# An attention step reordered: the latent product of the step behind moves up to the scores, the outputs move to the end

## The chip, the cores and the metric

The kernel runs on one core of a Trainium2 chip. The metric is device time in microseconds (us): 2148.81 us is the median of three runs of the kernel before. The core has a matrix engine (TensorE, PE in the rows; its weight loads are PEld), a vector engine (VectorE, DVE), a scalar engine (ScalarE, ACT), GpSimd (POOL) and a queue engine that only issues transfers (SyncE, SP). Each runs its own instruction stream in order and waits for the others on semaphores.

## What is computed

A front end of convolutions gives `h` (16 x 128 tokens of 1024). Then comes the part that the change touches, and then a feed-forward layer with low-rank experts. Cut to the attention:

```
q_c = rmsnorm(x @ w_qa);  q = q_c @ w_qb            # 32 heads, 128 plain + 64 rotary
k_c, k_rope = x @ w_kva;  k_c = rmsnorm(k_c)        # a latent of 128, shared by all heads
q_rope, k_rope = rotary(q_rope), rotary(k_rope)
scores = q_nope . k_nope + q_rope . k_rope          # per batch of 128 tokens and head
attn   = softmax(scores * 192**-0.5)
out    = attn @ v;  h = h + out @ w_o
```

The kernel never forms keys or values. It multiplies each head's query weight by its key weight beforehand (`wp`), and its value weight by its output weight (`m`); the scores are then taken against the latent `kc`, and `attn @ kc` (the latent product) is multiplied by `m` and added to `resid`. All matmuls work on fp16 pairs, a high part and a low part, so each product is three matmuls.

## The kernel before

The attention phase has 32 rounds of 4 steps, 128 steps `s`. A round is a group of 4 heads and a quad of 4 batches; a step is one batch j of the quad, for 4 heads at once. Each engine has a `body` for a round, written out by hand; the order within it is the order of the instructions. Rounds 1 to 26 run in a loop of two rounds a turn, rounds 28 to 30 in a loop of one; rounds 0, 27 and 31 stand alone. `more` is true for rounds 0 to 27.

In one step of before the engines do this.

- PE: `scores` of step s (12 matmuls of 128 columns against the latent, then 8 against the rotary keys, which wait for `zt`); `rope` of step s+1 (9 of 256 columns); `outputs` of step s-1 (24 of 512 columns into two banks); `queries` (9 of 512, one head of the next round); where `more` and j is 1 to 3, `products` (one third of the next group's weight product, in fp32); then the latent product of step s (3 of 512: `av_ps`), which waits for `turned`.
- DVE: the row maximum `mx` and its scaled negative `nmx`; `rotate` (4 instructions, `ra`, `rb`); `rrec` and the division of `prob`; the low half `z` of the rotary query; the low half of `halves`; two residual additions `add_out` for step s-1; `query_low`; `prod_low`; then `ot_l`, the low half of the latent product.
- ACT: at the start of a round the load of the next head's weights (`load`, line 858, 928 KB into `wide`); four exponentials `prob`; the high half of `z`; the high half of `halves`; `query_high`; `prod_high`; then `ot_h`, the high half of the latent product.
- SP: two DMA transposes a step, `zt` (`turn_rope`, the rotary queries of step s) and `turned` (`turn_prob`, both halves of the probabilities of step s). Both go on the SP queue, in the order of the code; the load goes on ACT's.

Single buffers tie the steps together: `halves`, `turned`, `av_ps`, `ot_h`, `ot_l`, `zt`, `z`, `s_ps` exist once. Registers that hold loop positions are worked out on PE's own sequencer, between the matmuls (rows `ISA` and `REGISTER_ALU` below).

Of the kernel before, what the change touches and what calls it, by code (L numbers as in the profile page):

```python
# [27 lines left out]
P = 128  # L28
# [706 lines left out]
def attention_phase(nc, keep, raw_loaded, heads_d):  # L735
# [3 lines left out]
    with ExitStack() as ctx:  # L739
# [60 lines left out]
        @block.sync  # L800
        def _(sp):
            def turn_rope(s):
                waits = [(z_lo, s + 1)]
                if not isinstance(s, int) or s >= 1:
                    waits.append((s_done, s))
                wait_apart(sp, sp_passed, *waits)
                sp.dma_start_transpose(zt[:, :, :], z[:, :, :].rearrange("p h n -> p (h n)")
                                       ).then_inc(zt_turned, 16)

            def turn_prob(s):  # L810
                waits = [(p_lo, s + 1)]
                if not isinstance(s, int) or s >= 1:
                    waits.append((av_done, s))
                wait_apart(sp, sp_passed, *waits)
                sp.dma_start_transpose(turned[:, :, :], halves[:, :]).then_inc(p_turned, 16)

            turn_rope(0)
            turn_prob(0)
            with sp.Fori(1, ROUNDS * QUAD) as s:
                turn_rope(s)  # L820
                turn_prob(s)

        @block.scalar
        def _(act):
# [45 lines left out]

            def body(before, now, after, more):
# [4 lines left out]
                for j in range(QUAD):  # L876
                    s = now.slot + j
                    act.wait_ge(max_step, s * 2 + 2)
# [24 lines left out]
        def _(dve):  # L903
# [61 lines left out]

            def body(before, now, after, more):
                for j in range(QUAD):
                    s = now.slot + j
                    dve.wait_ge(s_done, s + 1)
# [14 lines left out]
                    behind = (now, j - 1) if j else (before, QUAD - 1)  # L984
# [16 lines left out]
                if not after:  # L1001
                    for hf in range(2):
                        add_out(now, QUAD - 1, hf)
                    dve.wait_ge(out_added, ROUNDS * 8)
# [4 lines left out]
        def _(pe):  # L1009
# [103 lines left out]

            def body(before, now, after, more):
                operands = score_operands(now, 0)
                for j in range(QUAD):
                    s = now.slot + j
                    scores(now, j, operands)
                    if after or j < QUAD - 1:
                        if j < QUAD - 1:  # L1120
                            rope(now, j + 1)
                        else:
                            rope(after, 0)
                    if before or j:
                        if j:
                            outputs(now, j - 1)
                        else:
                            outputs(before, QUAD - 1)
# [4 lines left out]
                    if more and j:  # L1133
                        products(now.t + HEADS, now.parity, j - 1, prod_ps, (now.t + HEADS) * 3 + (j - 1))
                    if before or j:
                        pe.wait_ge(o_lo, s)
                    at = bass.ds(now.tok + j * P, P)
                    probs_h, probs_l = (turned[:, at, :].rearrange("p h n -> p (h n)")
                                        for at in (slice(0, HEADS), slice(HEADS, 2 * HEADS)))
                    pe.wait_ge(p_turned, s * 16 + 16)  # L1140
                    pe.matmul(av_ps[:, :], kc_h[:, at], probs_h, start=True, stop=False)
                    pe.matmul(av_ps[:, :], kc_l[:, at], probs_h, start=False, stop=False)
                    pe.matmul(av_ps[:, :], kc_h[:, at], probs_l, start=False, stop=True).then_inc(av_done, 1)
                if not after:
                    outputs(now, QUAD - 1)
# [354 lines left out]
```

## Time and profile before

| | us |
|---|---|
| median of 3 runs | 2148.81 (2148.19 to 2150.49) |
| the profiled execution | 2150.39 |
| its span, first to last instruction | 2148.6 |
| front end, up to the first scores | 518.33 |
| steady rounds 10 and 11 | 43.35 and 42.97 |
| rounds 28, 29, 30 (no weight products) | 43.11, 42.84, 42.39 |
| PE busy in the span | 1956.3 (91%) |

The attention phase begins at 518 us of the span and ends near 1907. The profiled execution lasted 1.8 us longer than its span, which is what lies before the first and after the last instruction. PE's busy time counts modelled ends of matmuls that overlap the next one, so waits of PE under 0.2 us don't show as idle; they do show in the distance between two starts.

### The profile page before, as it was taken

The page shows a single profiled execution, that of the slowest core. Times are in us where ns is not written, and L with a number is a line of the kernel's source. Part 1 is how long each engine was busy: PE and PEld are TensorE (multiplying, and loading weights), DVE is VectorE, ACT ScalarE, POOL GpSimd, SP SyncE. Part 2 cuts the span into 40 slices and gives each one's busy share as a digit, 9 for nine tenths or more (in the row PEclk, how much of TensorE's full clock was granted, in tenths as well). Part 3 has the DMA queues.
Part 4 walks back from the last instruction along what each step waited for, and adds up shares of the span by engine and source line. Part 5 has one row for each costly group of instructions (what it writes and reads, how often), then busy time and mean ns, then how long its engine had stood idle before and what let it go on. Part 6 is the DMA issues. An engine that isn't in the chain of part 4 may idle for free. (4 is left out here: it accounts for less than half of the span.)

```text
span 2148.6 us, 42567 instructions
## 1 busy us (share of the span) xinstructions
PE 1956.3 (91%) x11826; PEld 1066.0 (50%) x11826; DVE 1344.1 (63%) x2822; ACT 792.8 (37%) x2067; POOL 315.4 (15%) x612
## 2 busy tenths in 40 slices
PE   4688888866999999999999999999999999949999
PEld 1344444443555555555555555555555555525554
DVE  3666666654666666666666666666666666655664
ACT  3344444433333333333333333333333333332221
POOL 2355555430000000000000000000000000023332
PEclk8888888978999999999999999999999999979999
DMA  4111111102222222222222222222222121142332
GB/s 136 40 40 39 39 39 39 36 1 81 55 56 55 72 54 53 53 72 54 54 53 71 55 52 54 72 54 54 54 72 54 38 38 37 38 137 70 79 86 70
DMA packets 250560, 123.82 MB, mean 58 GB/s; under 512 B 240272, under 2 KB 240528, under 8 KB 248336
## 3 DMA queue, kind: packets, MB, share of 16 engines
q1 hardware_dynamic: 246192, 94.71, 20.2%
q10 hardware_dynamic: 4320, 28.51, 3.8%
q8 instruction: 25, 0.41, 0.1%
q14 instruction: 23, 0.19, 0.0%
HBM read 56.07 MB, written 8.39 MB: 30 GB/s over the span
## 5 line engine op out<-in xcount | busy, mean ns | idle before, releaser
L1101 PE MATMUL out_ps<-m_h,ot_h 128*128 (+1 forms) x1024 | 389.7, 381 | 8.1 <-issue 3.2
L1102 PE MATMUL out_ps<-m_l,ot_h 128*128 (+1 forms) x1024 | 388.9, 380 | 0.0
L1103 PE MATMUL out_ps<-m_h,ot_l 128*128 (+1 forms) x1024 | 388.8, 380 | 0.0
L882 ACT ACTIVATE prob<-s_ps,nmx 128x128 f32<-128x128 f32 x512 | 181.3, 366 | 234.6 <-DVE nmx L975 234.6
L826 ACT ACTIVATE qp_h<-qp_ps 128x512 f16<-128x512 f32 (+1 forms) x126 | 75.2, 597 | 481.0 <-PE qp_ps L1036 481.0
L955 DVE SCALAR_TENSOR_TENSOR resid<-out_ps,resid 128x512 f32 (+1 forms) x256 | 176.2, 688 | 83.6 <-PE out_ps L1103 83.6
L905 DVE SCALAR_TENSOR_TENSOR qp_l<-qp_ps,qp_h 128x512 f16<-128x512 f32 (+1 forms) x126 | 87.2, 692 | 225.6 <-ACT qp_h L826 225.6
L1291 POOL MEMSET fpower<- 128x1 f32 x1 | 0.1, 99 | 1421.1 <-POOLq L739 1421.1
L1101 PEld LDWEIGHTS out_ps<-m_h,ot_h 128*128 128x128 f16 x1024 | 100.2, 98 | 137.6 <-issue 25.4
L1103 PEld LDWEIGHTS out_ps<-m_h,ot_l 128*128 128x128 f16 x1024 | 100.4, 98 | 113.8 <-issue 0.9
L1102 PEld LDWEIGHTS out_ps<-m_l,ot_h 128*128 128x128 f16 x1024 | 100.1, 98 | 106.4 <-issue 0.8
L905 DVE SCALAR_TENSOR_TENSOR halves<-prob,halves 128x512 f16<-128x512 f32 x128 | 88.7, 693 | 59.6 <-ACT halves L826 59.6
L826 ACT ACTIVATE halves<-prob 128x512 f16<-128x512 f32 x128 | 80.7, 631 | 85.6 <-DVE prob L981 85.6
L882 ACT ACTIVATION_READ_ACCUMULATOR prob<-s_ps,nmx 128x1 f32 x512 | 103.9, 203 | 0.0
L905 DVE SCALAR_TENSOR_TENSOR ot_l<-av_ps,ot_h 128x512 f16<-128x512 f32 x128 | 87.7, 685 | 24.8 <-ACT ot_h L826 23.9
L1036 PE MATMUL qp_ps<-qct_h,wp_h 128*128 (+1 forms) x378 | 102.8, 381 | 0.0
L1036 PE MATMUL qp_ps<-qct_h,wp_l 128*128 (+1 forms) x378 | 102.2, 379 | 0.0
L1036 PE MATMUL qp_ps<-qct_l,wp_h 128*128 (+1 forms) x378 | 102.1, 379 | 0.0
L1079 PE MATMUL s_ps<-kct_h,qp_h 128*128 (+1 forms) x512 | 93.1, 220 | 5.8 <-DVE qp_l L905 3.2
L1404 PE MATMUL fout<-wb_h,fht_h 128*128 128x512 f16 x256 | 97.3, 380 | 0.0
L1404 PE MATMUL fout<-wb_l,fht_h 128*128 128x512 f16 x256 | 97.1, 379 | 0.0
L1404 PE MATMUL fout<-wb_h,fht_l 128*128 128x512 f16 x256 | 97.0, 379 | 0.0
(246 smaller groups left out, 4130.1 us busy)
## 6 DMA issues: line engine op xcount, KB each, us to landing
wide<-heads_in ACTq DMA_DIRECT2D x30, 928.0 KB, 4.6
wide<-x_in SPq DMA_DIRECT2D x32, 512.0 KB, 6.2
tower_out<-result SPq DMA_DIRECT2D x16, 512.0 KB, 2.6
stage<-wb_in SPq DMA_DIRECT2D x8, 512.0 KB, 8.2
resid<-wqk_in SPq DMA_DIRECT2D x1, 2304.0 KB, 10.8
zt<-z SPq DMA_TRANSPOSE x128, 2.4
turned<-halves SPq DMA_TRANSPOSE x128, 3.1
wide<-heads_in SPq DMA_DIRECT2D x2, 928.0 KB, 4.6
```

The costliest lines, as they stand in the source:

```text
L826: act.activation(out, src, ACT.Copy, scale=scale).then_inc(done, 1)
L882: act.activation(prob[:, h, :], s_ps[:, h * P:(h + 1) * P], ACT.Exp, bias=nmx[:, h:h + 1], scale=EXP_SCALE, accum_out=rsum[:, h:h + 1]).th ...
L905: dve.scalar_tensor_tensor(out=out, in0=src, scalar=scale, in1=high, op0=ALU.mult, op1=ALU.subtract).then_inc(done, 1)
L955: dve.scalar_tensor_tensor(out=resid[:, at], in0=out_ps[hf][:, :], scalar=1.0 / (O_S * M_S), in1=resid[:, at], op0=ALU.mult, op1=ALU.add). ...
L1036: last = pe.matmul(bank[:, :], w[:, bass.ds(side, 1), k, j, :].rearrange("p a n -> p (a n)"), q[:, k, bass.ds(tok, CHUNK)], start=n == 0, ...
L1079: pe.matmul(out[h], q_h[h], k_h, start=h == 0, stop=False)
L1101: pe.matmul(out_ps[hf][:, :], ot_h[:, h, :], m_h[:, at], start=h == 0, stop=False)
L1102: pe.matmul(out_ps[hf][:, :], ot_h[:, h, :], m_l[:, at], start=False, stop=False)
L1103: last = pe.matmul(out_ps[hf][:, :], ot_l[:, h, :], m_h[:, at], start=False, stop=h == HEADS - 1)
L1291: pool.memset(power[:, :], -0.5).then_inc(powered, 1)
L1404: pe.matmul(out_ps[p][hf][:, :], h[p][:, k, :], w[:, k, hf * CHUNK:(hf + 1) * CHUNK], start=k == 0 and n == 0, stop=False)
```

## The change

PE's step becomes: scores of s, latent product of s-1, `rope` of s+1, `queries`, `products`, `outputs` of s-1. On ACT `ot_h` of s-1 moves to the head of step s, before the exponentials; since the round's load stands before the steps, it now follows `prod_high` of the last step directly. On DVE `ot_l` of s-1 follows `nmx`, before `rotate`, and the two additions `add_out` come last. On SP the transpose of `zt` runs a step ahead: `zt` of s+1 and then `turned` of s, where it was `zt` of s and then `turned` of s.

```diff
 @block.sync
-            turn_rope(0)
-            turn_prob(0)
-            with sp.Fori(1, ROUNDS * QUAD) as s:
-                turn_rope(s)
+            turn_rope(0)
+            turn_rope(1)
+            turn_prob(0)
+            with sp.Fori(1, ROUNDS * QUAD - 1) as s:
+                turn_rope(s + 1)
                 turn_prob(s)
+            turn_prob(ROUNDS * QUAD - 1)
 @block.scalar
+            def latent_high(s, first):
+                act.wait_ge(av_done, s + 1)
+                if not first:
+                    act.wait_ge(out_done, s * 2)
+                high(ot_h[:, :, :].rearrange("p h n -> p (h n)"), av_ps[:, :], O_S / (PR_S * KC_S), o_hi)
...
                     s = now.slot + j
+                    if before or j:
+                        latent_high(now.slot + (j - 1), not before and j == 1)
                     act.wait_ge(max_step, s * 2 + 2)
...
-                    act.wait_ge(av_done, s + 1)
-                    if before or j:
-                        act.wait_ge(out_done, s * 2)
-                    high(ot_h[:, :, :].rearrange("p h n -> p (h n)"), av_ps[:, :], O_S / (PR_S * KC_S), o_hi)
 @block.vector
                     dve.tensor_scalar(nmx[:, :], mx[:, :], -EXP_SCALE, None, ALU.mult).then_inc(max_step, 1)
+                    if behind[0]:
+                        latent_low(now.slot + (j - 1))
                     if after or j < QUAD - 1:
                         rotate(s + 1)
...
-                    if behind[0]:
-                        add_out(*behind, 0)
-                        add_out(*behind, 1)
                     if after:
                         query_low(after, j)
                     if more and j:
                         prod_low(now.t + HEADS, now.parity, now.side * -1 + 1, now.place, j - 1, prod_ps)
-                    dve.wait_ge(o_hi, s + 1)
-                    low(ot_l[:, :, :].rearrange("p h n -> p (h n)"), av_ps[:, :], O_S / (PR_S * KC_S),
-                        ot_h[:, :, :].rearrange("p h n -> p (h n)"), o_lo)
+                    if behind[0]:
+                        add_out(*behind, 0)
+                        add_out(*behind, 1)
 @block.tensor
                     scores(now, j, operands)
+                    if behind[0]:
+                        latents(*behind)
...
                     if after:
                         queries(after, j)
+                    if more and j:
+                        products(now.t + HEADS, now.parity, j - 1, prod_ps, (now.t + HEADS) * 3 + (j - 1))
+                    if behind[0]:
+                        outputs(*behind)
                     if j < QUAD - 1:
                         operands = score_operands(now, j + 1)
```

On ACT, at the turn from the last step of a round to the next round, before; `m_h` is the last `prod_high`, and `wide` the tile that the load fills:

```order
L826 ISA [waits out_done,prod_done]
L826 ACTIVATE m_h<-prod_ps 128x512
L826 ACTIVATE ot_h<-av_ps 128x512 [waits out_done,av_done]
L873 ISA
L858 ISA [waits wr_lo,prod_done]
L858 DMA wide<-heads_in 128x1856
```

The same place now:

```order
L826 ISA [waits out_done,prod_done]
L826 ACTIVATE m_h<-prod_ps 128x512
L879 ISA
L858 ISA [waits wr_lo,prod_done]
L858 DMA wide<-heads_in 128x1856
L685 ISA
L874 ISA [waits av_done]
L826 ACTIVATE ot_h<-av_ps 128x512 [waits out_done]
```

The load no longer stands behind the wait for the latent product (`av_done`); that wait is now behind the load.

On PE, in the first step of a round (j = 0), from the wait for `turned` on, before:

```order
L1140 ISA [waits o_lo]
L1141 ISA [waits p_turned]
L1141 MATMUL av_ps<-turned,kc_h 128x512
...
L1143 MATMUL av_ps<-turned,kc_h 128x512
L685 ISA
L1067 ISA
L1075 REGISTER_ALU [waits qp_lo]
L1079 MATMUL s_ps<-kct_h,qp_h 128x128 [waits exp_done]
```

And now (`...` stands for the rest of the latent product and of the 9 `rope` matmuls, with 8 more register rows):

```order
L1132 ISA [waits p_turned]
L1132 MATMUL av_ps<-turned,kc_h 128x512
...
L685 ISA [waits rot_step]
L1063 ISA
L1063 MATMUL rope_ps<-wr_h,qct_h 128x256
...
L685 ISA [waits prod_lo]
L685 ISA [waits qp_lo]
L686 ISA
L1047 REGISTER_ALU
L1047 MATMUL qp_ps<-qct_h,wp_h 128x512
```

Behind the wait for `turned` there stood the scores; now there stand `rope` and `queries`, with their register rows.

On SP, the loop's body before, and then now:

```order
L807 DMA_TRANSPOSE zt<-z 128x4x128 [waits z_lo,s_done]
L815 DMA_TRANSPOSE turned<-halves 128x8x128 [waits p_lo,av_done]
L819 REGISTER_ALU
L819 COMPARE_AND_BRANCH
```

```order
L89 REGISTER_ALU [waits z_lo]
L806 DMA_TRANSPOSE zt<-z 128x4x128 [waits s_done]
L813 DMA_TRANSPOSE turned<-halves 128x8x128 [waits p_lo,av_done]
L818 REGISTER_ALU
L818 COMPARE_AND_BRANCH
```

The rows read alike, but the `zt` row now carries the step ahead, so within one step `zt` is issued in front of `turned` and not behind it.

## Rows read from the trace of the kernel before

**Rows 1.** Windows, a round or part each: from:to, length, busy (count) by engine, clock.

```profile
957.62:1000.97 43.35, 42.55 (x272) 23.47 (x271) 28.28 (x60) 16.44 (x54) 0.00 (x0) 1.00 0.26 58
1000.97:1043.94 42.97, 42.62 (x270) 23.41 (x271) 28.41 (x60) 16.10 (x52) 0.00 (x0) 1.00 0.26 59
1733.91:1777.02 43.11, 40.89 (x260) 22.09 (x261) 27.44 (x58) 15.13 (x49) 0.00 (x0) 1.00 0.20 38
1819.86:1862.25 42.39, 40.74 (x260) 22.12 (x261) 26.04 (x56) 14.52 (x48) 0.00 (x0) 1.00 0.20 37
1862.25:1892.61 30.36, 24.27 (x169) 13.72 (x170) 17.73 (x39) 8.55 (x33) 0.00 (x0) 1.00 0.21 39
```

**Rows 2.** Timeline of PE, steady rounds: start, length, line, operation, tiles, count.

```profile
904.48 0.22 PE L1086 MATMUL s_ps<-kr_l,zt 128*128 x1
904.53 0.49 PE L1052 MATMUL rope_ps<-wr_h,qct_h 128*128 x3
904.86 0.49 PE L1052 MATMUL rope_ps<-wr_l,qct_h 128*128 x3
...
911.46 0.81 PE L1036 MATMUL qp_ps<-qct_h,wp_l 128*128 x3
...
912.75 1.02 PE L1024 MATMUL prod_ps<-wide 128*128 128x512 f32 x2
913.61 0.38 PE L1141 MATMUL av_ps<-turned,kc_h 128*128 128x512 f16 x1
```

**Rows 3.** Timeline of ACT, DVE, SP and PE, one step of round 31 (brackets: idle before).

```profile
1872.51 0.60 ACT L826 ACTIVATE ot_h<-av_ps 128x512 f16<-128x512 f32 x1 [4.88 <-PE av_ps L1143]
1873.14 0.69 DVE L905 SCALAR_TENSOR_TENSOR ot_l<-av_ps,ot_h 128x512 f16<-128x512 f32 x1 [2.70 <-ACT ot_h L826]
1873.74 0.68 DVE L970 TENSOR_REDUCE mx<-s_ps 128x4 f32<-128x512 f32 x1
1874.46 0.17 DVE L975 TENSOR_SCALAR nmx<-mx 128x4 f32<-128x4 f32 x1
1874.61 0.42 DVE L937 TENSOR_TENSOR ra<-rope_ps,consts 128x256 f32<-128x256 f32 x1
1874.66 0.37 ACT L882 ACTIVATE prob<-s_ps,nmx 128x128 f32<-128x128 f32 x1 [1.56 <-DVE nmx L975]
1876.20 0.18 DVE L979 RECIPROCAL rrec<-rsum 128x4 f32<-128x4 f32 x1 [0.31 <-ACT prob L882]
1878.59 1.23 SPq L815 DMA_TRANSPOSE turned<-halves  x1
1881.81 0.38 PE L1141 MATMUL av_ps<-turned,kc_h 128*128 128x512 f16 x1 [2.06 <-DMA turned<-halves]
```

**Rows 4.** Timeline of ACT at a round's turn.

```profile
913.91 0.60 ACT L826 ACTIVATE m_h<-prod_ps 128x512 f32 x1 [0.36 <-PE prod_ps L1024]
914.46 0.60 ACT L826 ACTIVATE ot_h<-av_ps 128x512 f16<-128x512 f32 x1
915.06 0.34 ACTq L858 DMA_DIRECT2D wide<-heads_in  x1
```

**Rows 5.** Landing times of `turned`, of `zt`; two issues; packets, 519.5 to 523.2 us.

```profile
DMA to landing us min/median/max: 3.1/3.1/3.2
DMA to landing us min/median/max: 2.4/2.4/4.3
519.56 0.34 ACTq L858 DMA_DIRECT2D wide<-heads_in  x1
520.48 1.30 SPq L807 DMA_TRANSPOSE zt<-z  x1
q10 hardware_dynamic: 115, 0.85, 71.0%
```

**Rows 6.** Timeline of PE at the first step of round 11.

```profile
1002.74 0.49 PE L1052 MATMUL rope_ps<-wr_h,qct_l 128*128 x3
1003.47 0.39 PE L1101 MATMUL out_ps<-m_h,ot_h 128*128 x1 [0.23 <-issue]
```

More of the change, by code:

```diff
@@ L802, in turn_rope @@
             def turn_rope(s):
-                waits = [(z_lo, s + 1)]
+                wait_apart(sp, sp_passed, (z_lo, s + 1))
                 if not isinstance(s, int) or s >= 1:
-                    waits.append((s_done, s))
-                wait_apart(sp, sp_passed, *waits)
+                    wait_apart(sp, sp_passed, (s_done, s))
                 sp.dma_start_transpose(zt[:, :, :], z[:, :, :].rearrange("p h n -> p (h n)")
@@ L810, in turn_prob @@
             def turn_prob(s):
-                waits = [(p_lo, s + 1)]
+                wait_apart(sp, sp_passed, (p_lo, s + 1))
                 if not isinstance(s, int) or s >= 1:
-                    waits.append((av_done, s))
-                wait_apart(sp, sp_passed, *waits)
+                    wait_apart(sp, sp_passed, (av_done, s))
                 sp.dma_start_transpose(turned[:, :, :], halves[:, :]).then_inc(p_turned, 16)
             turn_rope(0)
+            turn_rope(1)
             turn_prob(0)
-            with sp.Fori(1, ROUNDS * QUAD) as s:
-                turn_rope(s)
+            with sp.Fori(1, ROUNDS * QUAD - 1) as s:
+                turn_rope(s + 1)
                 turn_prob(s)
+            turn_prob(ROUNDS * QUAD - 1)
         @block.scalar
@@ L894, in body @@
                         prod_high(now.t + HEADS, now.parity, now.side * -1 + 1, now.place, j - 1, prod_ps, False)
-                    act.wait_ge(av_done, s + 1)
-                    if before or j:
-                        act.wait_ge(out_done, s * 2)
-                    high(ot_h[:, :, :].rearrange("p h n -> p (h n)"), av_ps[:, :], O_S / (PR_S * KC_S), o_hi)
+                if not after:
+                    latent_high(now.slot + (QUAD - 1), False)
             rounds(act, start, body)
@@ L964, in start, with latent_low @@
                 rope_low(0)
+            def latent_low(s):
+                dve.wait_ge(o_hi, s + 1)
+                low(ot_l[:, :, :].rearrange("p h n -> p (h n)"), av_ps[:, :], O_S / (PR_S * KC_S),
+                    ot_h[:, :, :].rearrange("p h n -> p (h n)"), o_lo)
             def body(before, now, after, more):
@@ L968, in body @@
                     s = now.slot + j
+                    behind = (now, j - 1) if j else (before, QUAD - 1)
                     dve.wait_ge(s_done, s + 1)
@@ L983, in body @@
                                       ).then_inc(norm_step, 1)
-                    behind = (now, j - 1) if j else (before, QUAD - 1)
                     if after or j < QUAD - 1:
@@ L997, in body @@
                         prod_low(now.t + HEADS, now.parity, now.side * -1 + 1, now.place, j - 1, prod_ps)
-                    dve.wait_ge(o_hi, s + 1)
-                    low(ot_l[:, :, :].rearrange("p h n -> p (h n)"), av_ps[:, :], O_S / (PR_S * KC_S),
-                        ot_h[:, :, :].rearrange("p h n -> p (h n)"), o_lo)
+                    if behind[0]:
+                        add_out(*behind, 0)
+                        add_out(*behind, 1)
                 if not after:
+                    latent_low(now.slot + (QUAD - 1))
                     for hf in range(2):
@@ L1112, in start, with latents @@
                 rope(Round(pe, 0), 0)
+            def latents(r, j):
+                if not r.known or r.t or j:
+                    pe.wait_ge(o_lo, r.slot + j)
+                at = bass.ds(r.tok + j * P, P)
+                probs_h, probs_l = (turned[:, at, :].rearrange("p h n -> p (h n)")
+                                    for at in (slice(0, HEADS), slice(HEADS, 2 * HEADS)))
+                pe.wait_ge(p_turned, r.slot * 16 + (16 * j + 16))
+                pe.matmul(av_ps[:, :], kc_h[:, at], probs_h, start=True, stop=False)
+                pe.matmul(av_ps[:, :], kc_l[:, at], probs_h, start=False, stop=False)
+                pe.matmul(av_ps[:, :], kc_h[:, at], probs_l, start=False, stop=True).then_inc(av_done, 1)
             def body(before, now, after, more):
@@ L1116, in body @@
                 for j in range(QUAD):
-                    s = now.slot + j
+                    behind = (now, j - 1) if j else (before, QUAD - 1)
                     scores(now, j, operands)
[L1119 to L1128, printed above, removed]
+                    if behind[0]:
+                        latents(*behind)
+                    if j < QUAD - 1:
+                        rope(now, j + 1)
+                    elif after:
+                        rope(after, 0)
                     if after:
                         queries(after, j)
+                    if more and j:
+                        products(now.t + HEADS, now.parity, j - 1, prod_ps, (now.t + HEADS) * 3 + (j - 1))
+                    if behind[0]:
+                        outputs(*behind)
                     if j < QUAD - 1:
                         operands = score_operands(now, j + 1)
[L1133 to L1143, printed above, removed]
                 if not after:
+                    latents(now, QUAD - 1)
                     outputs(now, QUAD - 1)
```

## The prediction, made before the change was run

> **What bounds the kernel now.** I read the windows of single rounds first, then PE's starts inside a round, then one step's chain over the other engines, and last the transfers.
>
> The windows [rows 1] show PE near its limit. In rounds 10 and 11 it is busy 42.55 of 43.35 us and 42.62 of 42.97, at a granted clock of 1.00. The starts on PE [rows 2] say what a round would take without waits: a 128-column matmul follows its predecessor after 0.055 us (904.48 to 904.53), three of 256 columns take 0.33 (904.53 to 904.86), six of 512 take 1.29 (911.46 to 912.75), a product of 512 columns in fp32 takes 0.86 (912.75 to 913.61), the 384-column one about three quarters of that, 0.65. A step is then 20 score matmuls 1.10, rope 0.99, outputs 24 x 0.215 = 5.16, queries 1.94 and the latent product 0.65: 9.84 us. Four steps are 39.4, the products add 2.4: 41.75 us. The mean of the two steady rounds is 43.16, so PE loses 1.41 us a round. Rounds 28 and 30 have no products and still take 43.11 and 42.39 [rows 1], 3 us or more over 39.4. Nothing else comes close to being a bound: DVE is busy 28 us in such a round.
>
> PE loses this because the latent product of step s stands in step s and needs the whole chain of that same step: maximum, exponentials, division, split, transpose. One step of round 31 shows that chain with few other waits [rows 3]: the first exponential at 1874.66, `turned` issued at 1878.59, the latent product at 1881.81. PE idled 2.06 us before it.
>
> **What the change takes away.** The latent product of s-1 now comes behind the scores of s, so a chain that begins when the scores end has a step's other work as cover. I count from the end of a step's last score matmul, call that zero, and write lengths in us.
>
> The latent product of the step behind ends at about 0.65, and `ot_h` follows near 0.7. ACT's copies start 0.55 apart [rows 4], so the exponentials start at 1.25. `nmx` doesn't hold them: it comes 0.72 after the maximum starts and 0.20 ahead of the exponential (1873.74, 1874.46, 1874.66) [rows 3], which gives 1.0. `ot_l` starts 0.63 behind `ot_h`, at 1.33, and what follows it on DVE 0.60 later [rows 3], so `rotate` starts at 1.93. In the row `rotate` ran 0.05 before the exponential and DVE then idled 0.31 before `rrec` [rows 3]. Now `rotate` is 0.73 later against the exponential; 0.31 of that is covered and 0.42 is a new delay. From the exponential to the issue of `turned` the row has 3.93: 1.25 + 3.93 + 0.42 = 5.6. On SP `zt` of the next step now stands ahead. Its data is ready about 1.1 earlier (estimate: `z` is the DVE instruction ahead of `halves`), and its issue holds SP for 1.3 [rows 5], so `turned` goes out at about 5.85. PE starts 3.22 after that [rows 3]: 9.07.
>
> PE asks for it at the length of the step less 0.17: 9.67 in the first step of a round, 10.3 in the second, 10.5 in the other two. By this the wait is gone everywhere, with 0.6 us to spare at the tightest place. DVE's additions, now last, wait for the second output bank and finish during the scores (0.69 against 1.10), so the next maximum isn't held. PE's outputs find `ot_l` done at about 2.0, while they start after 3.4. Both cost nothing while that holds; without it each would cost some tenths a step.
>
> **What the change adds.** Two things, both at the turn of a round.
>
> First, the load of 928 KB. It was issued behind `ot_h`, late in the last step [rows 4]. Now it stands behind `m_h`. `m_h` starts 0.14 after the product's end (912.75 + 1.02 to 913.91) [rows 2, 4], and the product ends 0.65 + 0.99 + 1.94 + 0.86 after the scores' last issue, so `m_h` is released at about 4.6 and the load goes out up to 0.6 later [rows 4]: 4.9 to 5.2. That is just ahead of `turned` at 5.85. The trace holds one transpose that was issued just behind a load, 0.92 us behind (519.56, 520.48) [rows 5]. It landed after 4.3 where the median is 2.4, and until 523.2 only the load's queue q10 had moved packets [rows 5]: the transpose waited for the load to drain. Its landing came 5.2 after the load's issue. `turned` takes 0.7 more than `zt` (3.1 against 2.4), so it lands 5.9 after the load's issue, at 10.8 to 11.1, and PE needs another 0.14. Against 10.5 that is a wait of 0.4 to 0.7. What is left of `zt` may queue ahead of it too, up to 0.5 (half of it, an estimate). Call this term A: 0.4 to 1.2, I take 0.8.
>
> Second, PE's sequencer. It stops at the wait for `turned` and works out registers only after it. Before, 1.10 us of scores stood behind that wait; now `rope` and `queries` stand there with their register rows. In the first step of round 11 PE waited for issue between `rope` and the outputs: the last three of `rope` start at 1002.74 and are through at 1003.07, the outputs start at 1003.47 [rows 6], 0.40. The queries of the first step have five register rows ahead of them and no scores to hide them. Term B: 0.4 as in that row, up to 1.0; I take 0.8, nearer the top because the cover is shorter. It arises only where the landing is late; elsewhere the sequencer has the scores' time.
>
> The other 3 steps of a round have no load and no such term. The load stands in rounds 0 to 26; that of round 0 is where it was, so 26 turns have A + B.
>
> **The sum.** Steady rounds: A + B = 1.6 in place of 1.41, +0.2 x 26 = +5. Rounds 28 to 30 have no load: they go to 39.4 plus 0.3 for what is left, from a mean near 42.8: 3 x 3.1 = -9.3. Round 31 has no queries either; its steps took 30.36 for three [rows 1]. There the chain is a loop: `turned` to PE 3.22, latent product to `ot_h` 0.85, to the exponential 0.55, to the issue 4.6, together 9.2, so -2.6 for three steps, and +0.4 at its end, where the chain is longer. Rounds 0 and 27 gain what a steady round lost, an estimate of -1 each. Sum: +5 - 9.3 - 2.2 - 2 = -8.5. The profiled execution took 2150.4, which makes 2142; that execution is 1.6 above the median of the runs, so a median would be 2140 to 2142. I forecast 2142.
>
> A measurement of this kernel can tell a change of about 0.2%, 4.3 us.
>
> **Rivals.**
>
> *The load doesn't hold the transpose.* The two share the transfer engines and `turned` keeps moving beside the load. It then lands at most about 1.4 late (half of its 3.1, an estimate of its own moving time), at 10.4, and PE hardly waits: A 0, B about 0.2. So 26 x 1.2 = 31 us go and the rest of the sum stays: 2150.4 - 31 - 13.5 = 2106. For it: only one transpose in the trace shows the other behaviour, and `turned` is issued at a somewhat different moment. Against it: that one transpose, which moved nothing until the load was through [rows 5]. Chance 0.18. The Trainium skill (Trainium Kernel Development and Optimization, Key Constraints) states this rival as a rule: transfers from the SP and ACT queues run on the same 16 engines and interleave. By that rule the time would be the 2106 just worked out; the row at 520.48 doesn't agree with it.
>
> *The turn costs more than it saves: slower.* If all of `zt` and then `turned` queue behind the load, and the load goes out at 5.2, A is 1.3; with B at 1.0 the turn costs 2.3 against 1.41: +0.9 x 26 = +23, less 13.5: 2160. It decides from A + B = 1.41 + 13.5 / 26 = 1.93 on. For it: `zt` is issued only some 0.5 ahead of the load. Against: half of it should be through by then. Chance 0.22.
>
> *Nothing moves.* PE's losses are mostly issue, not the landing, and the new order keeps them: then steady rounds stay at 43.16 and only rounds 28 to 31 gain part of their 11 us, 2146. This lies inside the forecast's own range; I give it 0.05 of the forecast's chance.
>
> **How the numbers follow.** The forecast, A + B between 1.2 and 1.95, has 0.60: 26 x (-0.2 to +0.55) - 13.5 gives 2132 to 2151, 2142 in the middle. Three fifths of it lie under 2144.5, two fifths within 0.2%. Faster: 0.18 + 0.37 = 0.55; same: 0.23 and a little from the slower rival, 0.25; slower 0.20. The range reaches half way into both rivals, 2112 to 2160; I leave 0.1 below and 0.08 above.
>
> **What would show it.** In the changed profile the time from `turned`'s issue to landing at the last step of rounds 0 to 25 should be 4.5 to 5.5 where all others have 3.1, and PE's longest wait for `turned` should stand at the first step of rounds 1 to 26, 0.4 to 1.2 each, about 20 us in all. Behind it there should be waits for issue ahead of the first queries. In other steps PE should have no gap over 0.2. Rounds 28 to 30 should take 39.4 to 40. The prediction is wrong if `turned` lands after 3.1 everywhere (then 2106), if a steady step other than the first waits for it (the chain is longer than 5.85), or if DVE starts the maximum late because the additions hold it.

## The result and the profile after

The changed kernel takes 2156.21 us (median of 13 runs, 2152.26 to 2158.37); the kernel before, timed beside it, takes 2149.57 (13 runs, 2145.92 to 2152.33). The ratio is 1.0028, interval 1.0021 to 1.0035: slower by a little more than the 0.2% that can be told. The forecast was 2142, faster. The profiled execution took 2154.77 us, its span 2153.0 against 2148.6.

Windows of rounds 10, 11, 28 and 30 and of the first three steps of round 31, the same as in [rows 1]:

```profile
962.70:1006.74 44.04, 42.44 (x271) 23.63 (x270) 27.91 (x60) 15.72 (x52) 0.00 (x0) 1.00 0.26 58
1006.74:1050.51 43.77, 42.50 (x271) 23.64 (x270) 27.91 (x60) 15.81 (x52) 0.00 (x0) 1.00 0.25 58
1751.28:1791.03 39.75, 39.65 (x262) 22.13 (x261) 26.09 (x56) 14.11 (x48) 0.00 (x0) 1.00 0.24 41
1830.50:1869.98 39.48, 39.48 (x261) 22.08 (x260) 26.08 (x56) 14.11 (x48) 0.00 (x0) 1.00 0.21 40
1869.98:1897.17 27.19, 24.62 (x169) 13.71 (x168) 17.42 (x39) 9.13 (x33) 0.00 (x0) 1.00 0.18 35
```

The rounds without weight products went from 43.11 and 42.39 to 39.75 and 39.48, and round 30 has no wait left: PE is busy for all of it. The three steps of round 31 went from 30.36 to 27.19. The steady rounds went the other way, from 43.35 and 42.97 to 44.04 and 43.77. Over the program (from start to start of the rounds) rounds 1 to 26 lost 20.1 us; round 0 gained 3.3, round 27 0.6, rounds 28 to 30 9.6, round 31 3.9; 1.8 were lost outside the attention phase (its last addition ends at 1912.1 in before and at 1915.9 now). That sums to +4.4, the difference of the spans.

What PE waits for in most of the steady rounds (560 to 1720 us; total, times, longest):

```profile
PE qp_ps L1047 <- issue: 21.1, 28, 0.8
PE s_ps L1096 <- DMA zt<-z: 10.9, 24, 0.7
PE av_ps L1132 <- DMA turned<-halves: 5.2, 25, 0.3
```

Three waits, each about once a round. The timeline shows where: the turn from round 10 to 11, on SP, ACT and PE, the place of [rows 4] and [rows 6]:

```profile
1001.87 1.19 SPq L806 DMA_TRANSPOSE zt<-z  x1
1002.35 0.59 ACT L826 ACTIVATE m_h<-prod_ps 128x512 f32 x1
1002.47 0.35 ACTq L858 DMA_DIRECT2D wide<-heads_in  x1
1003.25 1.23 SPq L813 DMA_TRANSPOSE turned<-halves  x1
...
1007.36 0.22 PE L1092 MATMUL s_ps<-kct_h,qp_l 128*128 x1
1007.88 0.23 PE L1096 MATMUL s_ps<-kr_h,zt 128*128 x1 [0.30 <-DMA zt<-z]
...
1008.64 0.39 PE L1132 MATMUL av_ps<-turned,kc_h 128*128 128x512 f16 x1
...
1009.30 0.60 PE L1063 MATMUL rope_ps<-wr_h,qct_h 128*128 x3
...
1010.08 0.49 PE L1063 MATMUL rope_ps<-wr_h,qct_l 128*128 x3
1011.40 0.81 PE L1047 MATMUL qp_ps<-qct_h,wp_h 128*128 x3 [0.83 <-issue]
```

At this turn the load goes out 0.60 behind `zt` and 0.78 ahead of `turned`; in 13 of the 26 turns it is 0.59 to 0.65 behind `zt`, in the other 13 it is 0.28 or 0.29. The scores then wait for `zt`, the latent product for `turned` (1007.94 + 6 x 0.055 is the last score matmul's start, 1008.64 the next: 0.3 more than a matmul), and the queries for their registers. The other steps run at PE's pace, 10.54, 10.73 and 10.73 us, but for two early ones that took 11.06 and 11.48. The first step takes 11.55 to 12.26 where 9.87 would do.

Landing times of `zt`, of `turned` and of the load in the same stretch, min/median/max, for [rows 5]:

```profile
DMA to landing us min/median/max: 2.4/2.5/6.4
...
DMA to landing us min/median/max: 3.1/3.1/5.7
...
DMA to landing us min/median/max: 5.0/5.4/5.7
```

The long ones are those at the turns, 26 of `zt`, median 6.1, and 26 of `turned`, median 5.5, and three others (4.0 to 4.4). The load, landed after 4.6 before, takes 5.4.

The chain itself, one step of round 31, ACT and SP, beside [rows 3]:

```profile
1881.27 0.60 ACT L826 ACTIVATE ot_h<-av_ps 128x512 f16<-128x512 f32 x1 [5.34 <-PE av_ps L1134]
1881.77 0.36 ACT L890 ACTIVATE prob<-s_ps,nmx 128x128 f32<-128x128 f32 x1
...
1886.54 1.23 SPq L813 DMA_TRANSPOSE turned<-halves  x1
```

From the first exponential to the issue it is 4.77 now, 3.93 before.

### The profile page after: what moved, and what is told of

The parts are those of the page before. It is cut to its first block and busy times, and to the rows that moved or that the text cites. A ratio compares the mean times of both kernels' runs of the same rounds, so it can differ in the third digit from the quotient of the medians.

```text
span 2153.0 us, 42976 instructions
## 1 busy us (share of the span) xinstructions
PE 1947.8 (90%) x11826; PEld 1069.5 (50%) x11826; DVE 1331.6 (62%) x2822; ACT 776.8 (36%) x2067; POOL 314.9 (15%) x612
## 5 line engine op out<-in xcount | busy, mean ns | idle before, releaser
L826 ACT ACTIVATE ot_h<-av_ps 128x512 f16<-128x512 f32 x128 | 76.5, 597 | 762.1 <-PE av_ps L1134 762.1
L982 DVE TENSOR_REDUCE mx<-s_ps 128x4 f32<-128x512 f32 x128 | 88.5, 692 | 62.8 <-PE s_ps L1097 62.8
L1047 PE MATMUL qp_ps<-qct_h,wp_h 128*128 (+1 forms) x378 | 102.8, 381 | 21.1 <-issue 21.1
L890 ACT ACTIVATION_READ_ACCUMULATOR prob<-s_ps,nmx 128x1 f32 x512 | 109.0, 213 | 0.0
L588 PE MATMUL conv_ps<-wide,wc_h 128*128 128x512 f16 x256 | 78.8, 438 | 18.5 <-ACT wide L240 11.9
```

Source lines behind the costliest of these rows:

```text
L588: last = pe.matmul(conv_ps[c % 2][:, :], w[:, m, :], x[p][:, lo:lo + CHUNK], start=n == 0, stop=n == 3 * PAIRS - 1)
L826: act.activation(out, src, ACT.Copy, scale=scale).then_inc(done, 1)
L890: act.activation(prob[:, h, :], s_ps[:, h * P:(h + 1) * P], ACT.Exp, bias=nmx[:, h:h + 1], scale=EXP_SCALE, accum_out=rsum[:, h:h + 1]).th ...
L982: dve.tensor_reduce(mx[:, :], s_ps[:, :].rearrange("p (h n) -> p h n", h=HEADS), AX.X, ALU.max).then_inc(max_step, 1)
L1047: last = pe.matmul(bank[:, :], w[:, bass.ds(side, 1), k, j, :].rearrange("p a n -> p (a n)"), q[:, k, bass.ds(tok, CHUNK)], start=n == 0, ...
```

## The experiments

All are timed against the kernel before. The stretch for waits and landings is 560 to 1720 us throughout.

**The load moved behind the latent product's copy.** In the changed kernel the load went ahead only because `ot_h` moved away in front of it. Here it stands behind `ot_h` again, in the first step of a round.

```diff
-                if more and (not now.known or now.t + HEADS + 1 < NH):
-                    act.wait_ge(prod_done, now.t * 3 + 3 * HEADS)
-                    act.wait_ge(wr_lo, now.t + HEADS)
-                    load(now.t + HEADS + 1, 1 - now.parity)
...
                     if before or j:
                         latent_high(now.slot + (j - 1), not before and j == 1)
+                    if j == 0 and more and (not now.known or now.t + HEADS + 1 < NH):
+                        act.wait_ge(prod_done, now.t * 3 + 3 * HEADS)
+                        act.wait_ge(wr_lo, now.t + HEADS)
+                        load(now.t + HEADS + 1, 1 - now.parity)
```

> The changed kernel with one thing moved: the round's load is issued behind the high half of the latent product of the round's first step, and no longer ahead of it. Theory 1 (the load, issued ahead of the last step's two transposes, holds both until it has drained, and the landing and what PE's sequencer does behind it make the first step of rounds 1 to 26 about 2.05 us longer): the transposes land after 2.4 and 3.1 everywhere, the first step takes 9.9 to 10.0 in place of 11.8 to 12.1, a steady round 41.9 in place of 43.9, and the time falls by 26 x 2.0 = 52, to about 2104, which is 45 under the kernel before. Theory 2 (the first step is slow because of its register work behind the wait for the transposed probabilities, whatever the load does): the wait for issue ahead of the queries stays at 0.9, a steady round takes 42.9, and the time falls by the rest alone, 26 x 1.1 = 29, to 2127. Theory 3 (the additions at the end of the step or the longer chain cost the time): 2150 or more.

2116.46 us (2115.68 to 2118.46), ratio 0.9843 [0.9829, 0.9856]: 40 us less than the changed kernel, by this one edit. Its waits of PE, and then the landings of `zt` and of the load:

```profile
PE qp_ps L1047 <- issue: 10.4, 28, 0.7
```

```profile
DMA to landing us min/median/max: 2.4/2.4/4.3
...
DMA to landing us min/median/max: 4.4/4.6/4.8
```

Both waits for transposes are gone. One for issue is left, 0.38 and 0.71 in alternate rounds, with no late landing near it. That is most of what lies between 2104 and 2116: rounds of 42.24 and 42.56 against 41.87 without waits are 14 us over rounds 1 to 26.

**Less to load, at the changed kernel's place.** Twice the load keeps its place and issue, and moves fewer of its 1856 columns.

```diff
-            def load(h, p):
-                act.dma_start(raws[p][:, 0:RAW], heads_d[bass.ds(h, 1), :, :].rearrange("a p n -> (a p) n")
+            def load(h, p, cols=RAW):
+                act.dma_start(raws[p][:, 0:cols], heads_d[bass.ds(h, 1), :, 0:cols].rearrange("a p n -> (a p) n")
...
-                    load(now.t + HEADS + 1, 1 - now.parity)
+                    load(now.t + HEADS + 1, 1 - now.parity, 64)
```

> The changed kernel with the load where the change puts it, but of 64 columns a row in place of 1856 in rounds 0 to 26, so the weight products of those rounds work on the columns that an earlier load left. Theory 1 (what the load moves holds the transposes): a load of 1/29 holds them by 0.1 at most, the first step takes 9.9 to 10.0, and the time is that of the load moved away, 2104, give or take 4. If the place or the issue of the load on ACT mattered and not what it moves, the time stays near 2156. Theory 2 (register work alone): 2127.

> The changed kernel with every load of the loop cut to 928 of its 1856 columns (the weight products then use what stood in the other half, so the output is not the reference's; the instructions are the same). With the whole load the transposes at the turn land after 6.1 and 5.5, with 64 columns after 2.7 and 3.1. Theory 1 (the transposes land when the load has drained, so the hold goes with the bytes): the load lands after some 3.0, zt after 3.0 to 4.0 and turned after 3.1 to 3.5; both are then ahead of what PE asks for (a landing of up to 5.7 and 4.6), so only the issue wait of 0.4 to 0.7 is left: 2110 to 2117, as with 64 columns. Theory 2 (a load ahead of the transposes costs a fixed hold, whatever its size, and 64 columns only fall under some bound): 2140 to 2156.

With 64 columns 2111.65 us (2110.94 to 2113.01), ratio 0.9819 [0.9804, 0.9834]; with 928 columns 2115.18 (2111.72 to 2118.11), 0.9832 [0.9818, 0.9846]. Either way the waits for `zt` and `turned` are gone, though the load is issued from the same place. PE's list has one wait left, first with 64 columns, then with 928:

```profile
PE qp_ps L1047 <- issue: 10.6, 28, 0.7
```

```profile
PE qp_ps L1047 <- issue: 11.9, 28, 0.8
```

So the cost is what the load moves. The sizes give a series at the turn: load landed after 2.1, 3.9 and 5.4 us, `zt` after 2.7, 4.6 and 6.1, `turned` after 3.1, 4.0 and 5.5. With half a load, one turn:

```profile
902.17 1.19 SPq L806 DMA_TRANSPOSE zt<-z  x1
902.78 0.35 ACTq L858 DMA_DIRECT2D wide<-heads_in  x1
903.55 1.23 SPq L813 DMA_TRANSPOSE turned<-halves  x1
```

`zt` landed at 906.85, 0.26 after the load. In the changed kernel it is 0.24 to 0.28 after the load in all 26 turns. The theory of a fixed hold falls. The 2104 expected of 64 columns was missed by 8, by the same wait for issue as with the load moved.

**SP's order undone in the changed kernel**: `turned` and then `zt` of the next step.

```diff
-            turn_rope(0)
-            turn_rope(1)
-            turn_prob(0)
-            with sp.Fori(1, ROUNDS * QUAD - 1) as s:
-                turn_rope(s + 1)
-                turn_prob(s)
-            turn_prob(ROUNDS * QUAD - 1)
+            turn_rope(0)
+            turn_prob(0)
+            with sp.Fori(1, ROUNDS * QUAD) as s:
+                turn_rope(s)
+                turn_prob(s)
```

> The changed kernel with the order on SP of the kernel before: turned of a step, then zt of the step after (the run e4 only moved the end of SP's loop and left the order as changed). All else is the changed kernel, the load at the head of the round too. Theory 1 (a transpose that is not landed when the load goes out lands only when the load has drained): at the turn of a round both transposes are issued behind the load, zt now about 1.4 behind turned. Turned lands first, 10.4 to 10.9 after the scores, and zt about 1 later; the scores ask for zt at 10.3, so their wait grows from 0.25 to 0.77 to 1.0 or more, and the latent product's wait (0.3 to 0.4) goes. The wait for issue ahead of the queries (0.93) may shrink, since eight score matmuls and the latent product now stand between the late landing and them. Together a first step of 11.5 to 12.3 against 11.55 to 12.13: 2147 to 2165, with the whole wait at the scores. Theory 2 (what holds zt in the changed kernel is that it moves beside the load, and one issued behind turned is not held longer than before): the scores' wait stays at 0.6 or less and the latent product's goes too, 2135 to 2145.

2204.83 us (2198.16 to 2206.05), ratio 1.0245 [1.0230, 1.0261]. Both theories missed the size, though the place was that of theory 1:

```profile
PE s_ps L1094 <- DMA zt<-z: 44.6, 28, 2.2
PE qp_ps L1045 <- issue: 17.5, 24, 0.8
```

The scores wait 1.3 to 2.4 at each turn (distances between starts), and 0.6 to 1.0 in every step of rounds 28 to 30 but the very first, where no load runs: with `zt` 1.7 behind `turned` on the queue, it is late even when nothing else moves. So the order on SP is worth 48 us to the changed kernel. The wait for issue ahead of the queries did not shrink in 22 of the 26 turns (0.92 to 0.99): there the eight score matmuls and the latent product now behind the late landing hide none of it. In the other four it was 0.10 to 0.35; why in these alone stays open.

An earlier run (e4) was meant to undo the same order:

```diff
+            turn_rope(2)
-            with sp.Fori(1, ROUNDS * QUAD - 1) as s:
-                turn_rope(s + 1)
+            with sp.Fori(1, ROUNDS * QUAD - 2) as s:
                 turn_prob(s)
+                turn_rope(s + 2)
+            turn_prob(ROUNDS * QUAD - 2)
             turn_prob(ROUNDS * QUAD - 1)
```

> The changed kernel with only the order on SP undone: turned of a step is issued ahead of zt of the step after, as in before; all else is the changed kernel, the load at the head of the round too. Theory 1 (the landing of both transposes is held by the load, in the order of their issue): at the turn of a round turned lands first, zt some 0.5 to 1 behind it, and the scores stand ahead of the latent product on PE, so the scores' wait grows from 0.6 to 1.5 or more, while the latent product finds turned landed: the first step of a round gets 0.3 to 0.8 longer, 2164 to 2177. Theory 2 (zt's landing ahead is what costs, turned alone matters): the wait of the scores stays at 0.6 or less and the time is within 5 of the changed kernel's 2156.

It only moved the end of SP's loop to between the two transposes and left their order, so it tells nothing of either theory: 2152.92 us (2150.47 to 2154.03), ratio 1.0008 [0.9999, 1.0017]. `turned` goes out 1.7 behind `zt` in place of 1.4, and the load lands after a median of 5.2 in place of 5.4; that this is why it is 3 us faster than the changed kernel was not tried.

**SP's order alone, in the kernel before.**

```diff
-            turn_rope(0)
-            turn_prob(0)
-            with sp.Fori(1, ROUNDS * QUAD) as s:
-                turn_rope(s)
-                turn_prob(s)
+            turn_rope(0)
+            turn_rope(1)
+            turn_prob(0)
+            with sp.Fori(1, ROUNDS * QUAD - 1) as s:
+                turn_rope(s + 1)
+                turn_prob(s)
+            turn_prob(ROUNDS * QUAD - 1)
```

In this run SP also waits for the two semaphores of a transpose one after the other, as the changed kernel does.

> The kernel before with one part of the change alone: on SP the transpose of zt goes a step ahead of turned. PE's, ACT's and DVE's order is that of before, with the load behind the copy of the latent product. The load then stands behind both transposes of the step, so it holds neither: zt and turned should land after 2.4 to 2.7 and 3.1 to 3.4 everywhere. What is left: turned is issued up to 0.3 later, since zt is ahead of it on the queue, and the latent product of the same step waits for it. Theory 1 (PE loses in before because that latent product needs the whole chain of its step): no more than the same wait, 0 to 0.1 longer a step, 2149 to 2162. Theory 2 (the scores of the next step lose time to zt standing behind turned in before): that part of the 1.3 a round goes, 2135 to 2146.

2171.62 us (2169.64 to 2171.99), ratio 1.0096 [1.0080, 1.0111]. Theory 1 had the direction, and 2162 at most: the wait for `turned` went from 6.4 to 14.1.

```profile
PE av_ps L1141 <- DMA turned<-halves: 14.1, 28, 0.8
```

At the turns no transpose landed late (`zt` within 2.46, `turned` within 3.10); `turned` is merely issued later, by 0.20 to 0.36 at the median of each step, and before has no cover for that. The part that is worth 48 us in the new order costs 20 in the old.

**Rope ahead of the latent product on PE**, first in the changed kernel with its load, then with the load moved as above.

```diff
                     scores(now, j, operands)
-                    if behind[0]:
-                        latents(*behind)
...
+                    if behind[0]:
+                        latents(*behind)
                     if after:
                         queries(after, j)
```

> The changed kernel with the load as the change puts it, but on PE the rope product of the next step stands ahead of the latent product and not behind it, so 0.98 us more work covers the landing, and the register rows of rope are done ahead of the wait. Theory 1: the wait of the scores for the late rotary transpose (0.25 to 0.77) stays, the wait of the latent product (0.35) goes, and the wait for issue ahead of the queries falls from 0.93 to 0.2 or 0.3, since fewer register rows stand between the landing and the queries: the first step is longer by 0.7 to 0.9 and not by 2.05, 26 x 1.2 = 31 less, about 2125. Theory 2 (register work, however late the landing): the queries keep five register rows behind the wait, so 0.9 stays and only the latent product's 0.35 goes, 2147. Theory 3 (a longer chain costs): the latent product comes 0.98 later, so all steps lose, 2170 or more.

> The changed kernel with two edits: the load stands behind the copy of the latent product in the first step of a round (as in the run that took 2116), and PE takes the nine rope matmuls ahead of the latent product. With the load out of the way, the only wait of PE left in the steady rounds was for issue ahead of the first queries, 0.38 and 0.71 a round. Theory 1 (the sequencer does the register rows of rope only after the wait for turned): rope's rows are now done ahead of that wait, the issue wait shrinks to 0.2 or less, the chain starts 0.98 later but PE also asks 0.98 later, so the transposes still land in time: some 0.5 a round less over 28 rounds, 2100 to 2106. Theory 2 (the later copy of the latent product delays exponentials and transposes more than PE's own order gives back, as in the run of the changed kernel with rope ahead): a new wait for zt or turned of 0.3 or more a round, 2116 to 2130. If the issue wait belongs to the queries' own rows alone, it stays at 0.4 to 0.7 and the time is 2116.

With the load as changed: 2170.19 us (2167.93 to 2170.89), ratio 1.0090 [1.0075, 1.0106], 45 over theory 1. PE's waits:

```profile
PE s_ps L1096 <- DMA zt<-z: 35.4, 26, 1.6
PE qp_ps L1047 <- issue: 8.6, 26, 0.4
PE av_ps L1132 <- issue: 4.1, 13, 0.3
```

The wait for `turned` went, and of the 21.1 for issue 12.7 are left in two places. But the copy `ot_h` and all behind it come 0.98 later (the nine matmuls ahead of it). At the turn `zt` is issued 5.77 us after the last score matmul's start in place of 4.79 and the load 5.93 in place of 5.24 (medians); `zt` is held as in the changed kernel and lands about 1.0 later, while the scores ask for it when they did, and wait 0.9 to 1.8 (distances between starts). Theory 3 has the time, not the path: only the first steps lose, the others keep their 10.54, 10.73 and 10.73. With the load out of the way the same edit is neutral: 2116.19 (2115.21 to 2117.85), 0.9838 [0.9824, 0.9851], against 2116.46. The wait for issue stayed, most of it now behind the latent product, so it is not mainly `rope`'s rows that make it:

```profile
PE qp_ps L1047 <- issue: 7.4, 26, 0.4
```

**The queries' positions worked out ahead of the wait for `turned`**, again with the load as changed and with the load moved.

```diff
+            def query_operands(r, j):
...
+                if not r.known:
+                    for ap in (*ws[id(wp_h)], *qs[id(qct_h)], *ws[id(wp_l)], *qs[id(qct_l)]):
+                        pe.lower_ap(ap)
...
-                side, tok = fresh(pe, r.side, 1), fresh(pe, r.tok, TOK - QUAD * P)
+                ws, qs = operands or query_operands(r, j)
...
+                    ahead = query_operands(after, j) if after and j == 0 else None
                     if behind[0]:
                         latents(*behind)
...
-                        queries(after, j)
+                        queries(after, j, operands=ahead)
```

> The changed kernel with the load as the change puts it, but in the first step of each round the positions that the queries need are worked out between the scores and the latent product, ahead of the wait, and not behind it; some rows for the queries' own waits remain. This prices the second term by itself. Theory 1 (late landing and register work add up): the wait for issue of 0.93 falls to 0.3 or 0.5, the landing's waits stay, 26 x 0.5 = 13 less, about 2143. If the wait for issue only takes the place of another wait, the time stays at 2156.

> Two edits on the changed kernel: the load behind the copy of the latent product (as in the run that took 2116), and the positions of the first step's queries worked out on PE's sequencer ahead of its wait for turned (as in the run that took 2170). With the load out of the way no landing is late, and what was left of PE's waits was 0.38 and 0.71 for issue ahead of the first queries of a round, 14 in all. Theory 1 (that wait is the queries' own register rows behind the wait, and the waits for issue of 0.14 to 0.31 which the other steps then had in the run of 2170 came from its late landings): both go, rounds of 41.7 to 41.9, 2101 to 2106. Theory 2 (the positions worked out ahead cost the other steps register rows of their own): the first step falls to 9.9 to 10.0 but the other three gain 0.1 to 0.3 each, 2112 to 2128. If the wait has another cause, the first step keeps its 0.38 and 0.71: 2116.

With the load as changed: 2169.71 us (2167.58 to 2170.93), ratio 1.0087 [1.0073, 1.0100], against 2143 or 2156 expected. Most of the wait for issue went, and a longer one for `turned` stands there:

```profile
PE av_ps L1141 <- DMA turned<-halves: 27.8, 25, 1.5
```

This run shows something else besides. In 13 of its 26 turns the load goes out 0.92 to 1.17 behind `zt`. One of them, with the time from issue to landing:

```profile
1006.63 1.19 SPq L806 DMA_TRANSPOSE zt<-z  x1
1007.55 0.34 ACTq L858 DMA_DIRECT2D wide<-heads_in  x1
1008.01 1.23 SPq L813 DMA_TRANSPOSE turned<-halves  x1
...
zt<-z SPq DMA_TRANSPOSE x1, 2.5
turned<-halves SPq DMA_TRANSPOSE x1, 6.0
```

In all 13 `zt` landed after 2.44 to 2.46, as if no load ran; in the other 13, with the load 0.29 to 0.60 behind it, after 5.8 to 6.3. `turned`, behind the load, was held in all 26 (5.2 to 6.5).

With the load moved: 2150.80 (2147.74 to 2152.09), 1.0000 [0.9991, 1.0009]. PE's waits there, where no landing is late:

```profile
PE av_ps L1141 <- issue: 14.1, 26, 0.7
PE qp_ps L1057 <- issue: 1.2, 4, 0.5
```

Of theory 2 the part on the other three steps holds; the first step did not fall to 9.9 or 10.0 but takes 10.96, and the time is 23 over the theory's range. The wait of 0.38 and 0.71 ahead of the queries fell to 0.27, but the latent product now waits 0.57 and 0.84 for the same rows, and the other three steps gained 0.16 to 0.28 each, though nothing was moved there. The edit has a flaw that explains these: it works out the positions of all nine queries in one go, in every step, where they stood one by one between the matmuls (five register rows ahead of the first query in place of one). It doesn't price term B. It does show that four register rows gathered at one place cost about 0.2 us there, and that moving rows ahead of a wait only moves the stall.

## Why the prediction was wrong, by its own steps

**What bounds the kernel: in part.** The prediction put the whole loss of a steady round, 1.41, on the wait for `turned`. Against 41.87 without waits (the sum of the four steps at PE's pace) the loss is 1.30. By distances between starts in rounds 1 to 26, 0.38 of it is that wait, in the first step alone; 0.63 stands ahead of the outputs and 0.25 ahead of the next round's scores. PE's list of before, which leaves out short waits, has the same three:

```profile
PE av_ps L1141 <- DMA turned<-halves: 6.4, 14, 0.5
PE out_ps L1101 <- issue: 3.2, 13, 0.4
PE s_ps L1079 <- issue: 2.6, 12, 0.2
```

With the load moved a round takes 42.44, so the reordering by itself gives back 0.73 of the 1.30.

**The chain: right.** `turned` was worked out to go out 5.85 after the scores' end and goes out at 5.95 (in the first step of a round at 6.42); exponential to issue was 3.93 + 0.42 + 0.25 = 4.60, and is 4.77. In rounds 1 to 26 no step but the first waits for a transpose, but for one wait of 0.15.

**Rounds 28 to 31.** Rounds 28 to 30 were right: -9.3 forecast, -9.6 measured. The estimates beside them were short: round 31 -2.2 and -3.9; rounds 0 and 27 -2 and -4.0. Outside the attention phase 1.8 were lost that the forecast had not; that these parts come to -15.7 in all, near the -13.5 of the forecast, is in part luck.

**The turn: right in kind, too small.** The step that failed is "Steady rounds: A + B = 1.6 in place of 1.41". What stands there is 2.07 in place of 1.30 (means of rounds 1 to 26, 43.94 and 43.17, less 41.87). The sum was +5 for 26 rounds and is +20: 12 of the difference come from A + B, 3 from the 1.41; all other parts together came out 2 better than forecast. The 2.07 is made of three waits (distances between starts, first steps of rounds 1 to 26): scores for `zt` 15.3 us, 0.59 a round; latent product for `turned` 9.6 us, 0.37; queries for issue 24.8 us, 0.95, and 0.1 for the registers of `rope`.

Term A was 0.8 and is 0.96. Two of its inputs failed. "What is left of `zt` may queue ahead of it too, up to 0.5 (half of it, an estimate)": `zt`, issued 0.28 to 0.65 ahead of the load, is held whole; it lands after 6.1, just behind the load, and `turned` 1.0 behind the load. And the load was taken to drain in its old time of 4.6; beside the transposes it takes 5.4. The scores ask for `zt` ahead of the latent product, so a new wait stands where the prediction looked for none, and by the time it ends `turned` is nearly there. The small and the half load and the load moved show the cause: each removes both waits.

Term B was 0.8 and is 0.95 with the registers of `rope` beside it. "It arises only where the landing is late; elsewhere the sequencer has the scores' time" was wrong: with all landings in time 0.38 and 0.71 are left, 0.55 a round. About 0.4 of it hangs on the late landing. The traces show why: the five register rows ahead of these queries take 0.95 to 1.00 us on PE's sequencer, late landing or not. With the load moved they begin about 0.53 or 0.23 ahead of the start of the last `rope` matmul, in alternate rounds; in the changed kernel they begin 0.02 to 0.07 behind it. So the late landing takes away their lead, and they are seen at full length. No run took these rows away, so this is read from the traces alone.

**The rivals.** The slower one is what happened: its break-even was A + B = 1.93 and the turn costs 2.07, and `zt` and `turned` both come in behind the load. It put 2160 on A 1.3 and B 1.0. The rival of 2106, in which `turned` keeps moving beside the load and PE hardly waits, fails at all 26 turns; at the one shown in the last section the load's queue moved 92 packets in 2.2 us and the transposes' queue none. The Trainium skill (Trainium Kernel Development and Optimization, Key Constraints) says that transfers from the SP and ACT queues interleave; these packets don't agree. In the 13 turns with the load 0.28 or 0.29 behind `zt` the transposes' queue does move some 100 packets beside the load's (from 2.0 to 4.5 us after `zt`'s issue), and `zt` lands behind the load all the same. Another page of the Trainium skill (DMA: Bandwidth & Descriptors, Queues, rings and completion order) says that an engine drains a whole packet, there a bundle of descriptors, from one queue before it turns to the next. With that the packets of the turn shown agree, and the prediction had not weighed it; no run here shows the bundles themselves. The rival in which nothing moves was right that most of the loss is not the landing (0.92 of 1.30), and wrong that the new order keeps it: with the load moved 0.57 is left.

So the reordering is worth about 35 us as long as the load stays behind the copy (2116 against 2151 beside it). The changed kernel gave that back by one move: `ot_h` went to the head of the step, the load that had stood behind its wait went out early, between the two transposes.

## What to carry to other kernels

When a wait is moved on an engine that also issues transfers, look at which transfer was held back by it; here that was a load of 928 KB that nobody meant to move, and it cost 40 us. A small transfer on one queue needs a lead on a large one that goes out on another: here a lead of 0.92 us let `zt` land in its usual 2.45 though it was still on its way, and with one of 0.65 or less its landing has to be counted from the load's. What goes out behind the load is held in any case. Where PE runs near its limit, price its register rows as work: each place where they gather behind a wait cost 0.4 to 0.95 us, and moving them ahead of the wait moved the stall.

## What the hardware showed that was not expected

A transfer whose packets have all moved may still not land. Packets at the turn from round 10 to 11, by queue (q1 the transposes, q10 the load; packets, MB, share of the 16 engines), from 1001.8 to 1003.5, to 1004.1, to 1006.3 and to 1007:

```profile
q1 hardware_dynamic: 350, 0.09, 26.8%
...
q10 hardware_dynamic: 14, 0.10, 123.2%
q1 hardware_dynamic: 162, 0.04, 37.5%
...
q10 hardware_dynamic: 92, 0.68, 82.8%
...
q10 hardware_dynamic: 35, 0.16, 56.7%
q1 hardware_dynamic: 236, 0.05, 47.7%
```

350 + 162 = 512 packets of 256 bytes are the 128 KB of `zt`, and they had moved by 1004.1, ahead of most of the load; for 2.2 us after that the load moved alone. Yet `zt` landed at 1007.83, when the load had drained. The load ends with 16 packets of 4 bytes on q10 (1006.44 to 1007.10), and behind each of them two of 4 bytes follow on q1 within 0.02 us; the semaphore of `zt` rises 16 times after these (1007.60 to 1007.83). In 13 of the 26 turns all 512 had moved within 2.0 us of the issue; in the other 13 the last of them moved 4.7 to 5.0 after it. The landing came 0.24 to 0.28 after the load's in all 26.

The two sorts are the two leads: the 13 are the turns with the load 0.59 to 0.65 behind `zt`, the others those with 0.28 or 0.29. The run of 2170 with the queries' positions ahead adds a third sort. In its 13 turns with the load 0.92 to 1.17 behind, the last 4-byte packet of `zt` moves 2.05 to 2.09 after its issue and the load's first packet at 2.10 to 2.17, and `zt` lands in its usual time. With the load 0.58 to 0.60 behind, the load's first packet moves at 1.7, behind most of the data of `zt` and ahead of its 4-byte packets. By these turns it is the 4-byte packets that have to be ahead of the load. Why such small packets wait behind the load's, no run here shows.
